# Graph 1's edge messages: two of a group's eight chunks multiplied by their weights on ScalarE, head by head, instead of on VectorE

## What is computed

```python
h = (x @ W).reshape(N, H, C)                      # H = 8, C = 32
alpha = leaky_relu(a_src[src] + a_dst[dst], 0.2)
ex = exp(alpha - amax[dst])                       # amax: maximum over the edges of dst
denom = segment_sum(ex, dst)
attn = ex / (denom[dst] + 1e-16)
msg = h[src] * attn[:, :, None]
out = segment_sum(msg, dst).reshape(N, H * C) + bias
```

## Time and profile before

| | |
|---|---|
| median of three runs | 2640.28 us |
| lowest, highest | 2636.76, 2670.50 us |
| span of the profiled execution | 2267.9 us |
| TensorE, VectorE busy in it | 1862.7, 1730.8 us |
| ScalarE, GpSimd busy in it | 881.0, 1549.9 us |
| mean granted TensorE clock | 0.934 |

### The profile page before, as it was taken

How to read it: one execution, slowest core, us unless ns; L and a number is a source line. 1 busy time by engine, 2 the same in 40 slices (tenths; PEclk the granted TensorE clock), 3 DMA queues, 4 the chain that set the end, 5 groups by cost and what they waited for, 6 DMA issues and landing times.

```text
span 2267.9 us, 36390 instructions
## 1 busy us (share of the span) xinstructions
PE 1862.7 (82%) x10392; PEld 1202.2 (53%) x10392; DVE 1730.8 (76%) x4980; ACT 881.0 (39%) x2255; POOL 1549.9 (68%) x1715
## 2 busy tenths in 40 slices
PE   5677876688888788888667779999998999899817
PEld 3444444455555555555445556665655655555516
DVE  7689999899999999999679835656555665556568
ACT  3521111244444344444146534444443444433315
POOL 0477777777777777777755457777777777777710
PEclk9889998899999999999888879999999999999969
DMA  6444445444444444444640013333333233223279
GB/s 195 142 122 121 125 124 133 133 123 126 130 126 124 131 127 126 128 129 124 185 128 5 6 43 73 74 83 84 70 70 85 69 74 70 62 69 75 64 255 326
DMA packets 154492, 252.84 MB, mean 111 GB/s; under 512 B 39974, under 2 KB 79828, under 8 KB 154292
## 3 DMA queue, kind: packets, MB, share of 16 engines
q0 software_dynamic: 58624, 116.81, 22.1%
q1 hardware_dynamic: 95668, 133.66, 18.9%
HBM read 210.21 MB, written 40.15 MB: 110 GB/s over the span
## 4 chain that ended last, share of the span: by engine, by line
PE 36%; DVE 30%; issue 15%; POOL 11%; DMA 5%; DVEq 2%; ACT 1%; SPq 0%; ACTq 0%; POOLq 0%
PE pb L1331 11%; PE pb L1345 11%; DVE x_sb L2472 6%; PE pb L1422 4%; POOL Gb L754 3%; PE pb L1318 2%; DVE Gb L1642 2%; POOL tab L712 2%; DVE big L1606 2%; POOL early L754 2%; DVE x_sb L1865 2%; DMA early<-table,home 2%; DVE x_sb L2381 1%; DVE home L1642 1%; DMA Gb<-table,home 1%
## 5 line engine op out<-in xcount | busy, mean ns | idle before, releaser
L754 POOL DMA_INDIRECT Gb<-table,home x400 | 414.0, 1035 | 142.4 <-issue 105.4
L1345 PE MATMUL pb<-Gb,early 128*128 128x256 f32 x1568 | 395.2, 397 | 44.7 <-DVE home L2541 44.4
L1331 PE MATMUL pb<-big,Gb 128*128 128x512 f32 (+1 forms) x832 | 415.5, 615 | 10.2 <-DVE home L1766 9.6
L1318 PE MATMUL pb<-x_sb 128*128 128x394 bf16 x1024 | 299.8, 338 | 83.8 <-DVE x_sb L2472 79.7
L1345 PEld LDWEIGHTS pb<-Gb,early 128*128 128x128 f32 x1568 | 288.8, 194 | 131.8 <-DVE home L2541 57.4
L2472 DVE TENSOR_SCALAR x_sb<-iota,x_sb 128x394 bf16<-128x394 f16 x1024 | 345.9, 387 | 0.0
L831 ACT ACTIVATE early<-pb,b1c 128x512 f32<-128x512 f32 (+1 forms) x208 | 137.6, 662 | 397.5 <-PE pb L1331 397.2
L712 POOL DMA_INDIRECT home<-table,idx x224 | 221.1, 987 | 85.7 <-issue 64.4
L712 POOL DMA_INDIRECT tab<-table,idx x224 | 218.0, 973 | 68.3 <-issue 64.3
L1422 PE MATMUL pb<-Gb,Sall 128*128 128x264 f32 x800 | 247.5, 411 | 17.6 <-DVE Gb L1642 17.6
L821 ACT ACTIVATE x_sb<-pb 128x512 f16<-128x512 f32 x256 | 152.9, 597 | 275.3 <-PE pb L1310 274.9
(11 more groups left out here) (450 smaller groups left out, 3489.0 us busy)
## 6 DMA issues: line engine op xcount, KB each, us to landing
Sall<-dlT SPq DMA_DIRECT2D x180, 256.0 KB, 4.2
Y<-home SPq DMA_DIRECT2D x96, 256.0 KB
x_sb<-in_x_dram SPq DMA_DIRECT2D x8, 1536.0 KB, 15.2
big<-Y SPq DMA_DIRECT2D x12, 1024.0 KB, 10.8
Gb<-table,home POOLq DMA_INDIRECT x400
out_dram<-x_sb SPq DMA_DIRECT2D x24, 256.0 KB
Gb<-in_L_ffn_W_dram SPq DMA_DIRECT2D x8, 512.0 KB, 7.1
early<-Y SPq DMA_DIRECT2D x4, 1024.0 KB, 12.8
```

Of the source, the lines that this page charges most:

```text
L754: g.indirect_dma_start(out=G1[i % 4][:, k, :], out_offset=None, in_=g1.table, in_offset=bass.IndirectOffsetOnAxis(ap=g1.idx[:, c:c + 1], a ...
L1318: pe.matmul(pbank[5 + 2 * w][:, 0:HW], A, Bv[n], start=j % HB == 0, stop=j % HB == HB - 1).then_inc(p_pl, 1)
L1331: t = pe.matmul(pbank[b][:, 0:nt * 128], W1s[:, w, k, f * 128:f * 128 + 128], xT[:, t0:t0 + nt, k * 128:k * 128 + 128], start=k == 0, stop ...
L1345: t = pe.matmul(pbank[b][:, 0:D], hh[:, bi % 2, f, j * 128:j * 128 + 128], W2s[:, w, f, :], start=f == 0, stop=f == 3)
```

## The change

VectorE's `messages` is called for h = 0 to 2 (chunks 0 to 5) instead of 0 to 3. Chunks 6 and 7 are scaled in place on ScalarE, two heads a slot, by a new function `scaled`: chunk 6 in slots 4 to 7 of the iteration in which the group gets its weights, chunk 7 in slots 0 to 3 of the next. ScalarE's loop gets one iteration more for the last chunk 7. TensorE's sums wait for `v_msg` (now 3 a group) for chunks 0, 2 and 4, and for the new semaphore `a_msg` (2 a group) for chunks 6 and 7.

```diff
+            def scaled(e, c, h0):
+
+                if c == CG - 2 and h0 == 0:
+                    a.wait_ge(a_ex, e + 1)
+                for h in range(h0, h0 + 2):
+                    z = G1[e % 4][:, c, 32 * h:32 * h + 32]
+                    t = a.activation(z, z, ACT.Copy, scale=G1[e % 4][:, c, 256 + h:257 + h])
+                if h0 == 6:
+                    t.then_inc(a_msg, 1)
+
-            for i in range(NG1 + 1):
+            for i in range(NG1 + 2):
                 e = i - 1
-                if i >= 1:
+                if 1 <= i <= NG1:
                     a.wait_ge(p_tp, e + 1)
...
                 for k in range(CG):
-                    if k == 3 and i >= 1:
+                    if k < 4 and i >= 2:
+                        scaled(i - 2, CG - 1, 2 * k)
+                    if k == 3 and 1 <= i <= NG1:
                         a.wait_ge(v_z, 4 * e + 4)
                         a.activation(G1[e % 4][:, :, 256:264], z1b[:, e % 2, :, :], ACT.Exp).then_inc(a_ex, 1)
                     if k == 4 and i + 1 < NG1:
                         first_halves(i + 1)
+                    if k >= 4 and 1 <= i <= NG1:
+                        scaled(e, CG - 2, 2 * (k - 4))
...
-                        if k % 2 == 0:
-                            pe.wait_ge(v_msg, 4 * (i - 2) + k // 2 + 1)
+                        if k % 2 == 0 and k < CG - 2:
+                            pe.wait_ge(v_msg, 3 * (i - 2) + k // 2 + 1)
+                        if k >= CG - 2:
+                            pe.wait_ge(a_msg, 2 * (i - 2) + k - CG + 3)
...
-                        if k >= 4:
+                        if 4 <= k < 7:
                             messages(i - 1, k - 4)
```

More of the change, by code:

```diff
@@ L353, in build @@
         l_g = sems("l_g0 l_g1 l_g2 l_g3")
-        l_d1, s_dlT, v_oT, p_tp, a_w32, p_ad, v_z, a_ex, v_msg, p_sum, v_add = sems(
-            "l_d1 s_dlT v_oT p_tp a_w32 p_ad v_z a_ex v_msg p_sum v_add")
+        l_d1, s_dlT, v_oT, p_tp, a_w32, p_ad, v_z, a_ex, v_msg, a_msg, p_sum, v_add = sems(
+            "l_d1 s_dlT v_oT p_tp a_w32 p_ad v_z a_ex v_msg a_msg p_sum v_add")
         l_dr = sems("l_dr0 l_dr1")
```

## The result

In the runs that the comparison rests on, the changed kernel takes 2666.14 us (median of 20, 2643.87 to 2691.07) and the kernel before 2647.59 us (median of 20). The ratio is 1.0043, 95% interval 1.0022 to 1.0064: slower, by 11 us of 2647, where I had forecast 9 us less (by medians the difference is 19 us, of two sets of runs that scatter by 39 and 47 us). The time lies above my range (2600 to 2655).

What follows compares the result with a forecast made beforehand. The prediction took GpSimd's gathers to bound graph 1's edge loop, with VectorE near balance. Gains of 6 us (gathers) and 3 us (stall), ScalarE at 0, made 9 us less: 2640.3 - 9 = 2631 us, range 2600 to 2655.

Steps and rivals of the forecast that it cites:

- what lies around it (2640.3 - 2267.9 = 372.4 us to the median of the runs shown) stays: Profiled span to timed median: the 372.4 us between them was taken as unchanged, so the 9 us came off 2640.3.
- ScalarE's instructions: Graph 1's loop: 16 multiplications a group, one every 0.21 us, 3.4 us a group, 330 us in all, hidden: 0 us.
- The gathers are the pace: Graph 1's edge loop: GpSimd's gathers follow at the 0.30 us issue gap, never waiting but for 3.8 us.
- Gathers, 6 us gained: GpSimd's gathers (line 754): a quarter of line 1642's 24 us share of 73 us excess goes; bounds 0 to 18 us.
- The tail's 0.949 us: 1090 to 1149 us: 47 gathers without line 2472 average 0.949 us, near the floor, so line 1642 alone costs little.
- rival 1: Nothing comes of it: line 1642 doesn't slow gathers and the stall only moves; 2640 us; 20%.
- The stall, 3 us gained: Gather at 181.5 us waiting 4.08 us for TensorE's sum: fewer VectorE calls shorten it by 3 us; bounds 0 and 4.
- VectorE, 61 us less work, hidden: One messages call of 0.62 us goes in each of 98 groups; hidden behind the gathers, worth nothing directly.
- Rival 4: Dense stretch: ScalarE becomes the pace, its line 821 and TensorE's lookup waiting on each other; 45 us more, about 2680 us; 9%.
- Rival 2: Less packed VectorE frees gathers more than by share: 36 + 4 = 40 us gained, 2600 us; 12%.
- Rival 3: VectorE is the pace after all, its saving comes through in full: 61 us, 2579 us; 3%.
- The tail: Loop's end after the last gather: ScalarE delivers chunks 6 and 7 in time for TensorE's sums, hidden with 1 us to spare.

Runs made afterwards that it cites:

- condition B: Job-long state of timed runs, not chosen, in which the kernel before takes 2598 to 2671 us; the comparison's runs were in it.
- e14: VectorE multiplies only chunks 0 to 5, nobody 6 and 7 (constant summed instead), against the kernel before, in condition B: 2647.16 us, 1.0012.
- e13: VectorE multiplies all chunks, ScalarE's 16 copies a group go to an unread tile, against the kernel before, in condition B: 2658.04 us, 1.0038.
- A: Job-long state in which the kernel before takes 2268 to 2288 us; the profile ahead of the prediction was taken in it.
- e1: Kernel before, unchanged, profiled again in A: 2271.51 us, span 2269.7.
- e2: The changed kernel against the kernel before, in A: 2260.59 us, ratio 0.9908.
- e4: VectorE multiplies only chunks 0 to 5, nobody 6 and 7 (constant summed instead), against the kernel before, in A: 2259.01 us, 0.9900.
- e10: Same edit as e4, against the kernel before on another chip in A: ratio 0.9920, gathers busy 796.38 us.
- e12: As e4, with a one-input sum on VectorE in place of the fourth multiplication, against the kernel before, in A: 2265.80 us, 0.9953.
- e18: The changed kernel again, against the kernel before, in condition B: 2624.27 us, ratio 1.0033.
- e5: Kernel before, unchanged, profiled in condition B: 2623.32 us, span 2621.5.
- e3: VectorE multiplies all eight chunks, ScalarE's 16 copies a group go to an unread tile, against the kernel before, in A: 2280.44 us, 0.9981.
- e9: Same edit as e3, against the kernel before on another chip in A: ratio 0.9990, gathers busy 812.75 us.
- e16: As e13 with 24 copies of 32 columns a group instead of 16, against the kernel before, in condition B: 2633.88 us, 1.0068.
- e17: As e13 with 8 copies of 448 columns a group instead of 16 of 32, against the kernel before, in condition B: 2628.40 us, 1.0058.
- e7: The change with three chunks on ScalarE (5, 6, 7), against the kernel before, in condition B: 2644.03 us, 1.0113.
- e8: The change with four chunks on ScalarE (4 to 7), against the kernel before, in condition B: 2652.63 us, 1.0174.
- e15: The change with each slot's multiplications behind ScalarE's sort copies, against the kernel before, in condition B: 2651.93 us, 1.0034.

## Why the prediction was wrong

**The step that failed first: "what lies around it (2640.3 - 2267.9 = 372.4 us to the median of the runs shown) stays".** Nothing lies around a span but 2 us. The profile and the timed runs were of different conditions, and a gap of 372 us, 14% of the time, was the sign of it: in it the whole of condition B was hidden, and I carried it along as a constant. Every price in the sum was then read from a trace that doesn't describe the timed executions.

**The terms in the timed condition.** The two gains, 6 + 3 us, are worth nothing there (e14: 1.0012 [0.9986, 1.0037]), and ScalarE's instructions, which I put at 0 us, cost some 10 us (e13: 1.0038 of 2647 us). Together they give the wrong sign.

**The pace.** "The gathers are the pace" holds in A (e1, e2, e4). In B it fails, with 200 us of waits for TensorE's sums where the earlier trace rows has 38.5.

**Gathers, 6 us gained.** Right in mechanism in A, mis-sized: 14.8 us (e2 against e1; 15.5 by the means of four profiles each), near the upper bound of 18. I shared the excess of 73 us between lines 1642 and 2472 by busy time, a third to the first. The quarter of line 1642 that went took 14.8, so if the quarters are alike the line has 59 of the 73. The tail's 0.949 us misled me. The rule of the Trainium skill by which line 1642 is harmless (rival 1; SBUF — State Buffer, "Who interferes with whom") would leave the gathers as they are; in A e4 and e10 contradict it, and e12 adds that it isn't mostly the packed queue. What in a gather is held up, no run shows. In B the gathers of after and e18 are 2 to 5 us under e5's, and that is worth nothing.

**The stall, 3 us gained.** Not shown. At 181 us e1 has a gap of 1.17 us where the earlier trace rows have 4.08, e2 one of 2.30, e3 one of 5.63. It scatters from one execution to the next by as much as I priced it.

**VectorE, 61 us less work, hidden.** Hidden it was. By busy time it is 49 us in A (1730.1 to 1681.1), and VectorE then waits longer for landed gathers (55.8 us before line 1628 in e1, 80.7 before the same line, 1644, in e2). In B it hides behind TensorE.

**ScalarE's instructions.** The pitch was right: eight in a row take 1.81 us in e2, 0.21 us apart. In A they cost 0 us, three times over (e2, e3, e9), and TensorE waits for them for 0.2 us in all (e2). In the rows of ScalarE in e2 they stand in pairs between the sort's copies, beside waits for TensorE that stay (start, us, count, idle before):

```profile
700.75 0.60 ACT L821 ACTIVATE x_sb<-pb 128x512 f16<-128x512 f32 x1 [0.96 <-PE pb L1324]
701.24 0.52 ACT L943 ACTIVATE home<-home 128x32 f32<-128x32 f32 x2
701.98 1.01 ACT L953 CAST Sall<-pb 128x1024 f32<-128x1024 bf16 x1 [0.21 <-PE pb L1423]
```

In B it is a cost of 0.4%, some 10 us for 330 us of work on ScalarE. I had named the work that hides it (ScalarE's waits for TensorE) and the price if the cover is gone, a us a group for each us over. Neither is what happened. The cover isn't gone, ScalarE is busy for only 358.8 of 600 us, and still 3.4 us a group cost 0.1 us a group. My reading, not shown, is that where TensorE and ScalarE take turns irregularly, some hand-offs find ScalarE at work that it hadn't before. The runs show that more work on ScalarE costs more (e13, e16, e17, e7, e8) and that the order within a slot makes no difference that they can tell (e15), not the single delay.

**Rival 4** had the right queue, the right partner (line 821) and the right sign, but the wrong form: no engine at its limit, no threshold seen up to four chunks. Of its 45 us, some 10 came in B, and none in A. Rival 2 (36 us from the gathers, a mean gather under 1.0 us) is out in size, but in A its direction was right: the mean is 1.018 us in e2, less than my share gives (805.4/784 = 1.027). Rival 3 is out, no 61 us.

**The tail** stayed hidden (e2: the last 16 multiplications start at 1137.36 us beside VectorE's last three and end within TensorE's 10.5 us of sums).

## What to carry to other kernels

Set the span of the profile against the time of the run before anything else: if they differ by more than a few us, the profile is of another condition than the timings, and it can't price an edit. Before idle time under issue is read as an engine with nothing to do, count how many semaphore updates the trace has: a wait whose end isn't recorded looks the same. Work moved to an engine with slack was free here where one engine set the pace, and cost a small part of itself where several engines took turns. An edit that helps in one condition and hurts in the other is worth measuring in both.

## What the runs showed of the hardware

The same program takes 2279 us in one job and 2620 us in another on the same chip (2). On chip 12 its profile then has TensorE idle for 247 us more than in A, of which 66.1 us before products that wait for nothing (none in A), among them products 2.80 us apart where A has eight in 0.35 us, and a mean granted clock of 0.883 instead of 0.929. A third of the semaphore updates of VectorE and ScalarE are missing from that trace. In A, a multiplication of 128x512 numbers on VectorE lengthens GpSimd's gathers by 0.15 us for each that is done (14.8/98), and a sum of the same length with one input by a third of that or less (801.5 us in e12, where none has 796.4 to 800.4).
